# Gated experts: scaling the inner values by gate rows, and one PSUM sum over 34 pairs

## The reference

```
gu = x @ shared_gate_up_w
shared = _silu(gu[:, :Is]) * gu[:, Is:] @ shared_down_w
shared = shared * jax.nn.sigmoid(x @ shared_gate_w)
probs = jax.nn.softmax(x @ gate_w)
w, idx = jax.lax.top_k(probs, TOP_K)          # TOP_K = 8 of E = 64
w = w / jnp.sum(w, axis=-1, keepdims=True)
...                                           # at most 64 tokens per expert are kept
gu_e = jnp.einsum('ech,ehf->ecf', buf, expert_gate_up_w)
act = _silu(gu_e[..., :I]) * gu_e[..., I:]    # I = 64, Is = 256
out_e = jnp.einsum('eci,eih->ech', act, expert_down_w)
y = out_e[e_flat, slot] * w_flat[:, None]     # zero where dropped, then summed over the 8
return (y + shared).reshape(B, S, H)
```

## Time and profile before

| | |
|---|---|
| median of 3 runs | 4797.91 us |
| the profiled execution's own time | 4793.56 us |
| its span, first to last instruction | 4791.7 us |
| TensorE busy | 4050.0 us, 85% |
| VectorE busy | 3436.7 us, 72% |
| ScalarE busy | 2225.4 us, 46% |
| DMA queue of SyncE | 100.28 MB, 8.6% of 16 engines |
| the gated experts' stage | 3951.5 to 4151.9 us, 200.4 us |

### The profile page before, as it was taken

The page is one execution under the profiler, slowest core; times in us unless marked ns, Lnnn a source line. Parts: engine busy times, 40 slices in busy tenths (PEclk is TensorE's granted clock), DMA queues, the critical chain, the costliest instruction groups (busy, mean ns, idle before and its releaser), DMA issues. The chain is left out here.

```text
span 4791.7 us, 86667 instructions
## 1 busy us (share of the span) xinstructions
PE 4050.0 (85%) x24901; PEld 2629.4 (55%) x25261; DVE 3436.7 (72%) x17352; ACT 2225.4 (46%) x7299; POOL 396.3 (8%) x322
## 2 busy tenths in 40 slices
PE   8999999999999998938888888888874349789797
PEld 6888888888888887622333333333332235423356
DVE  6888888888888888547677777777764449744443
ACT  4555555555555555415555555555553212133232
POOL 0000000000000000020111111111100000023310
PEclk9999999999999999958888888888886559899998
DMA  0000000000000000122222222212210001100001
GB/s 29 2 2 2 2 2 2 2 2 2 2 2 2 2 2 2 34 60 52 48 52 48 52 48 52 45 44 47 44 33 5 4 1 38 35 10 11 8 14 40
DMA packets 80809, 105.31 MB, mean 22 GB/s; under 512 B 25599, under 2 KB 73914, under 8 KB 78395
## 3 DMA queue, kind: packets, MB, share of 16 engines
q1 hardware_dynamic: 80379, 100.28, 8.6%
HBM read 69.17 MB, written 30.26 MB: 21 GB/s over the span
## 5 line engine op out<-in xcount | busy, mean ns | idle before, releaser
L287 DVE CUSTOM_DVE_ANT_0 I-219junk<-I-215encw,I-218expo,I-227rec 128x77 f32<-128x77 f32 x3072 | 941.2, 356 | 6.3
L1315 DVE TENSOR_REDUCE I-41383nmax<-ps 128x1 f32<-128x512 f32 x768 | 500.9, 684 | 215.9 <-PE ps L984 209.4
L1203 ACT ACTIVATE I-41386prob<-ps 128x512 f32<-128x512 f32 x768 | 428.4, 596 | 227.8 <-PE ps L1021 145.7
L265 ACT ACTIVATE I-217tanh_s<-ps 128x77 f32<-128x77 f32 x1024 | 241.3, 236 | 595.1 <-PE ps L245 595.1
L245 PE MATMUL ps<-I-212hist,I-49small 128*128 128x77 f32 x2048 | 456.5, 305 | 40.7 <-DVE I-212hist L323 40.6
L245 PEld LDWEIGHTS ps<-I-212hist,I-49small 128*128 128x128 f32 x2048 | 305.0, 188 | 296.4 <-DVE I-212hist L323 296.3
L251 PE MATMUL ps<-I-217tanh_s,I-49small 128*128 128x77 f32 x2048 | 454.8, 304 | 0.0
L252 PE MATMUL ps<-I-212hist,I-49small 128*128 128x128 f32 x2048 | 440.0, 297 | 0.0
L247 PE MATMUL ps<-I-212hist,I-216uh_h 128*128 128x128 f32 x2048 | 439.8, 296 | 0.0
L984 PE MATMUL ps<-I-41377kS,I-41376qS 96*128 96x512 bf16 x768 | 331.2, 457 | 127.8 <-DVE I-41383nmax L1315 58.7
L273 ACT ACTIVATE I-223hh<-I-229gate_t,I-228pre,I-222rh 128x1 f32<-128x1 f32 x1024 | 395.3, 386 | 84.6
(11 more groups left out here) (534 smaller groups left out, 7254.4 us busy)
## 6 DMA issues: line engine op xcount, KB each, us to landing
I-41376qS<-parts SPq DMA_DIRECT2D x24, 768.0 KB, 7.5
parts<-I-41395room SPq DMA_DIRECT2D x36, 384.0 KB, 2.5
parts<-I-41395room SPq DMA_DIRECT2D x36, 256.0 KB, 2.2
I-41377kS<-parts SPq DMA_DIRECT2D x12, 768.0 KB, 7.9
parts<-I-41395room SPq DMA_DIRECT2D x36, 128.0 KB, 1.8
I-49small<-in_layers SPq DMA_DIRECT2D x6, 768.0 KB, 9.0
I-66646w<-in_blocks SPq DMA_DIRECT2D x8, 514.0 KB, 7.1
I-41376qS<-I-41385mrow SPq DMA_DIRECT2D x192, 2.0 KB
```

Source lines behind the costliest of these rows:

```text
L287: return e.tensor_tensor_reduce(junk[:, 2 * g + b, :], encw[:, g, b, :], expo[:, b, :], inv[:, b:b + 1], rec[:, b, g:g + 1], ALU.mult, ALU ...
L1203: e.activation(prob[:, tau % 2, j, :], k.ps[:, b, :], ACT.Exp, scale=scale).then_inc(free[b], 1)
L1315: e.tensor_reduce(nmax[:, U % HG, i, j:j + 1], k.ps[:, use[0], :], AX.X, ALU.max, negate=True).then_inc(free[use[0]], 1)
```

## The change

Only `gated_experts` is changed.

- The gates are turned at the start: TensorE transposes the 8 tiles of 128 tokens x 68 experts into PSUM, ScalarE copies them to `gT` (68 rows of 1024 tokens), and SyncE writes `gT` to a table in DRAM, `gates_rows`.
- For each pair SyncE fetches two rows of it, one expert's row over partitions 0 to 63 and the other's over 64 to 127, by two DMAs of 256 KB, into one of three buffers (`spread`).
- VectorE multiplies `hid` by `spread` in place, two instructions of 128x512 per pair between SBUF tiles. The 16 multiply-and-adds per pair are gone.
- The inner values now carry the gates, so TensorE sums both experts of a pair in one matmul over all 128 rows, 8 in place of 16, and all 34 pairs in the same two PSUM banks (`total`). VectorE adds `total` to `acc` once, at the end, in two instructions of 128x512.
- `sil` has two buffers, the loops are written out (a straight program), and all waits are on constants. The stage has 17 semaphores instead of 10.

```diff
--- before.py
+++ after.py
@@ -509,111 +509,107 @@
 def gated_experts(nc, k, nT, acc, gates, blocks):
...
     with ExitStack() as ctx:
         w = [sbuf(ctx, nc, f"w{u}", [P, 3 * P]) for u in range(GU)]
-        sil = sbuf(ctx, nc, "sil", [P, B * T])
-        lead = sbuf(ctx, nc, "lead", [P, 16])
+        sil = [sbuf(ctx, nc, f"sil{u}", [P, B * T]) for u in range(2)]
         hid = [sbuf(ctx, nc, f"hid{u}", [P, B * T]) for u in range(2)]
...
-        down = [k.ps[:, 4:6, :], k.ps[:, 6:8, :]]
...
-            with e.Fori(0, NPAIR // GU) as turn:
...
-        with stage(nc, "gate up act hidden down summed " + " ".join(f"load{u}" for u in range(GU))) as (block, s):
+        spread = [sbuf(ctx, nc, f"spread{u}", [P, B * T]) for u in range(3)]
+        gT = sbuf(ctx, nc, "gT", [2 * NPAIR, B * T])
+        gates_dram = nc.dram_tensor("gates_rows", (2 * NPAIR, B * T), F32).ap()
+        gate, up, total = k.ps[:, 0:2, :], k.ps[:, 2:4, :], k.ps[:, 4:6, :]
+        turned = k.ps[0:2 * NPAIR, 6:8, :]
+        with stage(nc, "turned kept sent gate up act product hidden down summed "
+                       + " ".join(f"load{u}" for u in range(GU)) + " rows0 rows1 rows2") as (block, s):
             load = [s.load0, s.load1, s.load2, s.load3]
+            rows = [s.rows0, s.rows1, s.rows2]
             @block.sync
             def _(e):
...
-                with e.Fori(0, NPAIR // GU - 1) as turn:
...
+                def fetch(n):
                     e.dma_start(w[n % GU][:], blocks[n]).then_inc(load[n % GU], 16)
+                def fetch_rows(n):
+                    src = gates_dram[2 * n:2 * n + 2, :].unsqueeze(0).to_broadcast([64, 2, B * T])
+                    e.dma_start(spread[n % 3][0:64, :], src[:, 0, :]).then_inc(rows[n % 3], 16)
+                    e.dma_start(spread[n % 3][64:128, :], src[:, 1, :]).then_inc(rows[n % 3], 16)
+                for n in range(GU):
+                    fetch(n)
+                e.wait_ge(s.kept, B)
+                e.dma_start(gates_dram, gT[:]).then_inc(s.sent, 16)
+                e.wait_ge(s.sent, 16)
+                for n in range(3):
+                    fetch_rows(n)
+                for n in range(3, NPAIR):
+                    e.wait_ge(s.hidden, B * (n - 2))
+                    fetch_rows(n)
+                    if n + 1 >= GU and n + 1 < NPAIR:
+                        e.wait_ge(s.down, n + 2 - GU)
+                        fetch(n + 1)
             @block.tensor
             def _(e):
...
+                for i in range(NT):
+                    mm = e.transpose(turned[:, i // TPB, (i % TPB) * P:(i % TPB + 1) * P], gates[:, i, :], k.ident)
+                    if i % TPB == TPB - 1:
+                        mm.then_inc(s.turned, 1)
+                def hidden(n):
+                    e.wait_ge(load[n % GU], 16 * (n // GU + 1))
                     for b in range(B):
...
+                        if n:
+                            e.wait_ge(s.act, B * (n - 1) + b + 1)
+                        e.matmul(gate[:, b, :], w[n % GU][:, 0:P], nT[:, b * T:(b + 1) * T], start=True, stop=True).then_inc(s.gate, 1)
+                        if n:
+                            e.wait_ge(s.product, B * (n - 1) + b + 1)
+                        e.matmul(up[:, b, :], w[n % GU][:, P:2 * P], nT[:, b * T:(b + 1) * T], start=True, stop=True).then_inc(s.up, 1)
+                def down(n):
                     for b in range(B):
...
-                        e.wait_ge(s.summed, 16 * n + (8 * b + 8))
...
-                                mm = e.matmul(tile(down[x], i), hid[u % 2][64 * x:64 * x + 64, i * P:(i + 1) * P],
-                                              w[u][64 * x:64 * x + 64, 2 * P:3 * P], start=(i % TPB == 0), stop=True,
-                                              skip_group_check=True)
...
+                        e.wait_ge(s.hidden, B * n + b + 1)
+                        for i in range(TPB):
+                            mm = e.matmul(total[:, b, i * P:(i + 1) * P], hid[n % 2][:, b * T + i * P:b * T + (i + 1) * P],
+                                          w[n % GU][:, 2 * P:3 * P], start=(n == 0 and i == 0), stop=(n == NPAIR - 1),
+                                          skip_group_check=True)
+                    mm.then_inc(s.down, 1)
+                hidden(0)
+                for n in range(NPAIR):
+                    if n + 1 < NPAIR:
+                        hidden(n + 1)
+                    down(n)
             @block.scalar
             def _(e):
...
+                for b in range(B):
+                    e.wait_ge(s.turned, b + 1)
+                    e.activation(gT[:, b * T:(b + 1) * T], turned[:, b, :], ACT.Copy).then_inc(s.kept, 1)
+                for n in range(NPAIR):
                     for b in range(B):
...
+                        e.wait_ge(s.gate, B * n + b + 1)
+                        if n >= 2:
+                            e.wait_ge(s.product, B * (n - 2) + b + 1)
+                        e.activation(sil[n % 2][:, b * T:(b + 1) * T], gate[:, b, :], ACT.Silu).then_inc(s.act, 1)
             @block.vector
             def _(e):
...
+                for n in range(NPAIR):
                     for b in range(B):
...
+                        cols = slice(b * T, (b + 1) * T)
+                        e.wait_ge(s.up, B * n + b + 1)
+                        e.wait_ge(s.act, B * n + b + 1)
+                        if n >= 2:
+                            e.wait_ge(s.down, n - 1)
+                        e.tensor_tensor(hid[n % 2][:, cols], sil[n % 2][:, cols], up[:, b, :], ALU.mult).then_inc(s.product, 1)
                     for b in range(B):
...
-                                e.scalar_tensor_tensor(acc[:, i, :], tile(down[x], i),
-                                                       gates[:, i, column:column + 1] if isinstance(n, int) else
-                                                       gates[:, i, bass.ds(column, 1)],
-                                                       acc[:, i, :], ALU.mult, ALU.add).then_inc(s.summed, 1)
...
-                    e.memset(lead[:, i:i + 1], 0.0).then_inc(s.summed, 1)
...
+                        cols = slice(b * T, (b + 1) * T)
+                        e.wait_ge(rows[n % 3], 32 * (n // 3 + 1))
+                        e.wait_ge(s.product, B * n + b + 1)
+                        e.tensor_tensor(hid[n % 2][:, cols], hid[n % 2][:, cols], spread[n % 3][:, cols], ALU.mult).then_inc(s.hidden, 1)
+                e.wait_ge(s.down, NPAIR)
+                for b in range(B):
+                    a = acc[:, TPB * b:TPB * (b + 1), :]
+                    e.tensor_tensor(a, a, total[:, b, :].rearrange("p (i d) -> p i d", d=D), ALU.add).then_inc(s.summed, 1)
```

More of the change, by code:

```diff
@@ L515, in gated_experts @@
         w = [sbuf(ctx, nc, f"w{u}", [P, 3 * P]) for u in range(GU)]
-        sil = sbuf(ctx, nc, "sil", [P, B * T])
-        lead = sbuf(ctx, nc, "lead", [P, 16])
+        sil = [sbuf(ctx, nc, f"sil{u}", [P, B * T]) for u in range(2)]
         hid = [sbuf(ctx, nc, f"hid{u}", [P, B * T]) for u in range(2)]
-        gate, up = k.ps[:, 0:2, :], k.ps[:, 2:4, :]
-        down = [k.ps[:, 4:6, :], k.ps[:, 6:8, :]]
-        tile = lambda ps, i: ps[:, i // TPB, (i % TPB) * P:(i % TPB + 1) * P]
-        def run_pairs(e, pair):
-            with e.Fori(0, NPAIR // GU) as turn:
[L526 to L529, removed]
@@ L546, in _ @@
             @block.tensor
             def _(e):
-                def hidden(n, u, before):
-                    e.wait_ge(load[u], (n - u) * (16 // GU) + 16)
-                    for b in range(B):
[L551 to L556, removed]
@@ L575, in _ @@
+                hidden(0)
[3 more added lines that the diff above has]
+                    down(n)
             @block.scalar
             def _(e):
-                def silu(n, before):
+                for b in range(B):
+                    e.wait_ge(s.turned, b + 1)
+                    e.activation(gT[:, b * T:(b + 1) * T], turned[:, b, :], ACT.Copy).then_inc(s.kept, 1)
+                for n in range(NPAIR):
                     for b in range(B):
[L579 to L582, removed]
@@ L591, in hidden @@
                     for b in range(B):
[L592 to L599, removed]
-                    for b in range(B):
-                        e.wait_ge(s.down, 2 * n + (b + 1))
-                        for x in range(2):
-                            for i in range(TPB * b, TPB * (b + 1)):
-                                e.wait_ge(s.summed, 16 * n + (8 * b + 4 * x + i % TPB + (13 if x else 5)))
-                                column = 2 * n + x
-                                e.scalar_tensor_tensor(acc[:, i, :], tile(down[x], i),
-                                                       gates[:, i, column:column + 1] if isinstance(n, int) else
-                                                       gates[:, i, bass.ds(column, 1)],
-                                                       acc[:, i, :], ALU.mult, ALU.add).then_inc(s.summed, 1)
@@ L613, in _ @@
```

(6 more changed lines are left out.)

19 lines of the change are left out of this document (removed).

## The result

The change takes 4780.96 us, the median of 7 runs (4778.46 to 4784.71), against 4797.91 for the kernel before in the same 7 rounds. The ratio is 0.9967, with a 95% interval of 0.9956 to 0.9979. That is 17 us less, and between 10 and 21 by the interval. The profiled execution took 4781.63 us with a span of 4779.9.

The account below looks back on a forecast made before the run. TensorE was taken to bound the stage by a hair over VectorE. Steady part -12.3, start +0.3, end -4.5 and barrier +0.5 summed to -16.0 us, giving 4781.9 us; range 4774 to 4796, own range 4777 to 4788.

Parts of the forecast that it names:

- Steady part: Middle 31 pairs: TensorE's pair falls from 5.616 to 5.22 us with 8 full-height down matmuls, gaining 12.3 us.
- the lower bound of 5.9 us: Middle pairs: if the waits between hidden matmuls stay, only 0.19 us per pair is gained on the down matmuls.
- Start: Stage up to the first regular pair: gate transposes, table write and first row fetches add 0.3 us, bounds -1.9 and +5.6.
- The cover of 2.1: Pair 0: gate products done by 3960.5, its down matmuls began at 3962.60, 2.1 us later, so nothing is late.
- Clock at the start: TensorE's first matmuls: earlier transposes might shorten half-speed work by 1.7 us or lengthen it by 2.8; taken as 0.
- End: After the last pair's first hidden matmul: two adds replace 32 multiply-and-adds, 13.23 us becomes 8.7, gaining 4.5.
- Barrier: Between VectorE's end and the next stage: seven more semaphores at 0.07 us each add 0.5 us, bounds 0 and 0.5.
- VectorE's and ScalarE's covers: Middle pairs: VectorE's gate products finish 2.9 us before their down matmuls; ScalarE's silus are as before, with two buffers.
- Rival (1): Middle: the pair keeps its 5.62 us through shared waits or slower program supply; -3.7 us left, 4794.2; chance 0.14.
- (3): Middle: gates are applied but the sum gains only the down part, 5.9 instead of 12.3 us; 4788.3; chance 0.14.
- Rival (2): Middle: row transfers become the bound, VectorE's gate product waits, 8.25 us per pair, 4875.9; chance 0.10.
- The 410 GB/s of the first load: Transfer rate seen in the kernel's first load, set against the 138 GB/s needed per pair, so transfers were costed at nothing.

Follow-up runs that it names:

- `onehalf`: Changed kernel with 64-row down matmuls for only the first expert of each pair; hidden matmuls took 3.63 us, the 8 down matmuls 1.98.
- `onetile`: Changed kernel with only one of the eight down tiles per pair split into two 64-row matmuls; 4795.13 us, a pair of 5.61 us.
- `twotiles`: Changed kernel with two of eight down tiles per pair split into 64-row matmuls, 128-row ones between them; 4818.00 us in one run, a pair of 6.00.
- `split`: Changed kernel with the 68-row gate table written by two transfers, 64 and 4 rows, instead of one; 4776.35 us in its one run.
- `straight`: Kernel before, with its loops written out for all 34 pairs and all waits on constants; 4798.59 us, ratio 1.0001.

## Why the prediction was right, point by point

The time was forecast as 4781.9 and is 4780.96. That is closer than the sum deserves: the stage and its barrier gave -13.8 where -16.0 was forecast, and the medians -17. The 2.4 us by which the start was mis-sized were made good by chance, by some 3 us outside the stage, which vary from one execution to the next.

- Steady part, -12.3 forecast, -12.27 measured. Right in size, wrong in part of its cause. The prediction had 0.19 us for 8 matmuls in place of 16 and 0.2 for the change of shape. `onehalf` shows that the number was worth nothing, and `onetile` and `twotiles` that the whole 0.39 us is the visit to 64-row work. Half of it falls on the hidden matmuls (3.63 against 3.43: 0.10 at the first one behind the visit, 0.09 at the last one ahead of it) and half inside the 1.98. The forecast came out right because the dense stage's row has neither, since it never leaves 128 rows. The rule cited from the Trainium skill, TensorEngine Tiling (Array Packing), Key Properties, holds in both its clauses: tiles work in parallel, and a change of mode drains. The words "the trace has 1.98 against 1.79", set against the parallel tiles, were the error: the 0.19 between them was drain too. So the lower bound of 5.9 us, the 0.19 as a gain from fewer matmuls alone, had nothing behind it.
- Start, +0.3 forecast, +2.73 measured, within the bounds of -1.9 and +5.6. The term was mis-sized twice. The write of `gT` was taken at 2.2 us from 256 KB stores and took 5.6; the first fetch was taken at 2.9 and took 5.0. Together 10.6 us where 5.1 were allowed. The cover of 2.1 was counted to the second gate product, while the first down matmuls wait only for the first, 0.7 us sooner, so it was 2.8, and 10.6 - 5.1 - 2.8 = 2.7 of the 3.0 us late are explained. `split` shows 2.4 us to be the shape of the write. The rule of the Trainium skill, DMA: Bandwidth & Descriptors, which had stood beside the sum, was on the right side, and the estimate from it, some 0.8 us late (2.7 - 2.1 would be 0.6), was still short of 3.0.
- Clock at the start: taken at 0, and it is. The first fast matmul comes 3.5 us after the first hidden one (3958.51 to 3962.02), as before (3953.87 to 3957.36). The transposes ahead of it did not bring it forward, and the clock did not fall again in the 3.0 us for which TensorE waited for the rows: the next pair runs at a granted clock of 1.00.
- End, -4.5 forecast, -4.74 measured. Barrier, +0.5 forecast, 1.77 - 1.27 = +0.50 measured.
- VectorE's and ScalarE's covers held; in the middle both only wait for TensorE.
- Rival (1), a pair that keeps 5.62 us, and (3), a gain of 5.9 alone, are out: the pair is 5.22, and `straight` excludes the program's form.
- Rival (2) did not happen, but the cover it was measured against was wrong. The 410 GB/s of the first load are not to be had for rows over 64 partitions, only 229. The point from which it decides, a pair of 5.74 us, was put at 126 GB/s, which is right for 721 kB. So 229 against 126 is a margin of 1.8, where 410 had given 3.3. The bound seen in the 9.0 us of 768 KB, about 87 GB/s, is not one for these transfers either.

## What to carry to other kernels

When two engines are both full, work out the pace of each alone in the new form, from a stage that already has that form. Freeing VectorE was the visible half of this change and brought nothing until TensorE's own pair got shorter. In a loop that mixes 64-row and 128-row matmuls, count the visits to the 64-row form and not the matmuls in it. And a new table on the way into a loop has a latency that no steady state hides: give its write a row count that splits well (64 and 4 took 3.2 us, 68 took 5.6), and ask for the first rows before anything else needs them.

## What the runs showed of the hardware

- A visit to 64-row matmuls between 128-row ones, in float32 at the high clock, costs 0.39 us, whether 2, 8 or 16 matmuls are in it, and two visits cost 0.78. Half of it is inside the visit, half on the 128-row work around it, and the first weight load behind a change runs in the open.
- Rows of 4 KB fetched from DRAM over 64 partitions arrive at 227 to 229 GB/s with the DMA engines full, where the first load with a 7 KB row over 128 partitions and plain tiles ran at 410. From one SBUF partition over 64 they arrive at 29 GB/s.
- 16 matmuls over 64 rows, two row groups in turn, took 1.98 us, and 8 over one group 1.98 as well.
- 68 rows of 4 KB were written to DRAM in 5.6 us (5.1 to 6.2 in seven traces), and the same rows as 64 and 4 in 3.2 and 3.4.
- From VectorE's last instruction to the next stage passed 0.65 us with 1 semaphore, 1.27 with 10, 1.77 with 17 and 1.84 with 18, which is about 0.07 us for each.
